# Moving the second graph linear layer into the next iteration, and the first norm's subtract-and-scale from VectorE to GpSimd

## The reference

```python
h = jnp.maximum(_layernorm(x, axis=-1), 0.0)
x = x + _L0_gnn_ref(h, L0_gnn_W, adj)      # qkv = h @ W; softmax(q k / sqrt(32) + mask) @ v
h = jnp.maximum(_layernorm(x, axis=-1), 0.0)
x = x + _L1_gnn_ref(h, adj, ...)
# in _L1_gnn_ref:
h = relu(adj @ (x @ Wg0 + bg0))
h = relu(adj @ (h @ Wg1 + bg1))
for p in range(1, 5):                      # windows of p tokens, an LSTM of p steps with its own weights
    last = _lstm_last(Wih[p - 1], Whh[p - 1], ..., wins)
    h = h.at[:, idx, :].set(last)          # replaces the last token of every window
```

## Time and profile before

| | us |
|---|---|
| median of 3 runs | 555.82 (555.24 to 557.22) |
| the profiled execution, its whole time | 555.92 |
| its span, first to last instruction | 554.1 |
| first phase up to the LSTMs' bulk | about 0 to 302 |
| one iteration of the loop, k = 4 to 13 | 17.58 |
| PE busy, DVE busy, ACT busy, POOL busy in the span | 500.2, 444.8, 352.1, 103.6 |

### The profile page before, as it was taken

The page is one execution under the profiler, slowest core; times in us unless marked ns, Lnnn a source line. Parts: engine busy times, 40 slices in busy tenths (PEclk is TensorE's granted clock), DMA queues, the critical chain, the costliest instruction groups (busy, mean ns, idle before and its releaser), DMA issues.

```text
span 554.1 us, 10019 instructions
## 1 busy us (share of the span) xinstructions
PE 500.2 (90%) x3464; PEld 433.8 (78%) x3464; DVE 444.8 (80%) x974; ACT 352.1 (64%) x573; POOL 103.6 (19%) x123
## 2 busy tenths in 40 slices
PE   3787999999999999999989999999999999999654
PEld 3577888888888888888778778889999988888533
DVE  4777888888888888887775788888788888788896
ACT  2446766677667766687557777777666676655341
POOL 2111110101111110100000012112111212233473
PEclk9989999999999999999999999999999999999975
DMA  7323000000000000000000000000000000000234
GB/s 214 101 82 90 2 2 1 1 0 0 0 0 0 0 0 0 0 0 2 1 0 1 2 0 2 0 0 2 1 1 1 1 0 1 0 2 17 60 95 133
DMA packets 18777, 11.28 MB, mean 20 GB/s; under 512 B 662, under 2 KB 17724, under 8 KB 18748
## 3 DMA queue, kind: packets, MB, share of 16 engines
q1 hardware_dynamic: 17052, 10.03, 6.3%
q10 hardware_dynamic: 1696, 0.87, 0.6%
HBM read 6.70 MB, written 4.19 MB: 20 GB/s over the span
## 4 chain that ended last, share of the span: by engine, by line
PE 52%; DVE 27%; ACT 11%; issue 7%; DMA 2%; DVEq 1%; POOL 0%; ACTq 0%; SPq 0%
PE ps L876 18%; PE ps L814 10%; DVE arena L1179 4%; PE ps L724 4%; DVE rmax L1098 4%; ACT arena L553 4%; DVE S_hi L1173 3%; PE ps L746 3%; PE ps L735 3%; DVE arena L1160 3%; DVE arena L1100 3%; PE ps L756 3%; PE ps L827 2%; PE ps L832 2%; ACT arena L575 2%
## 5 line engine op out<-in xcount | busy, mean ns | idle before, releaser
L589 ACT ACTIVATE arena<-ps,bias 128x512 f32<-128x512 f32 (+1 forms) x207 | 120.7, 625 | 38.3 <-PE ps L876 36.8
L553 ACT ACTIVATE arena<-ps 128x512 f32<-128x512 f32 (+1 forms) x112 | 87.6, 796 | 35.2 <-PE ps L735 20.7
L876 PE MATMUL ps<-H_hi,W_hi 128*128 128x512 f32 (+2 forms) x207 | 76.0, 367 | 6.5 <-DVE S_lo L1175 5.2
L724 PE MATMUL ps<-ident,arena 128*128 128x128 f32 x384 | 55.3, 293 | 29.3 <-ACT arena L558 16.3
L724 PEld LDWEIGHTS ps<-ident,arena 128*128 128x128 f32 x384 | 46.6, 150 | 40.4 <-ACT arena L558 22.8
L814 PEld LDWEIGHTS ps<-arena 128*128 128x128 f32 x512 | 69.0, 193 | 10.6 <-issue 5.3
L533 POOL TENSOR_TENSOR arena<-arena 128x512 f32<-128x512 f32 (+1 forms) x36 | 44.1, 1225 | 168.1 <-ACT arena L589 168.1
L876 PE MATMUL ps<-H_lo,W_hi 128*128 128x512 f32 (+2 forms) x207 | 75.3, 364 | 0.0
L876 PE MATMUL ps<-H_hi,W_lo 128*128 128x512 f32 (+2 forms) x207 | 74.9, 362 | 0.0
L814 PE MATMUL ps<-arena 128*128 128x33 f32 x512 | 66.1, 265 | 3.2 <-ACT arena L553 2.5
L558 ACT ACTIVATE arena<-arena 128x1024 f32<-128x1024 f32 x32 | 34.6, 1081 | 46.9 <-DVE arena L1100 46.9
(11 more groups left out here) (105 smaller groups left out, 1005.8 us busy)
## 6 DMA issues: line engine op xcount, KB each, us to landing
X<-in_x_dram SPq DMA_DIRECT2D x16, 256.0 KB, 2.8
out_dram<-X SPq DMA_DIRECT2D x14, 256.0 KB, 2.3
out_dram<-X ACTq DMA_DIRECT2D x2, 256.0 KB, 3.0
arena<-in_L_gnn_W_dram ACTq DMA_DIRECT2D x1, 128.0 KB, 3.1
wg<-in_L_gnn_Wg_dram ACTq DMA_DIRECT2D x2, 64.0 KB, 2.4
bg_rows<-in_L_gnn_bg_dram SPq DMA_DIRECT2D x6, 0.5 KB
wv<-in_L_gnn_W_dram ACTq DMA_DIRECT2D x1, 64.0 KB, 3.1
adj_sb<-in_adj_dram SPq DMA_DIRECT2D x1, 64.0 KB, 3.3
```

Source lines behind the costliest of these rows:

```text
L553: a_.activation(to, psum, func).then_inc(ready, 1)
L589: a_.activation(to[:, it.buf, 0:w], ps[:, 4 * it.par + j, 0:w], func, bias=bias[:, col:col + 1])\
L724: last = nc.tensor.transpose(to[:, b * P:(b + 1) * P], src[:, b, :], ident[:])
L876: l = mm(o, wt, v, start=m == 0, stop=m == len(terms) - 1)
```

## The change

The second graph linear layer leaves the end of iteration k. It is done in iteration k+1, behind the V and Q projections and ahead of the transposes of the probabilities; `graph_linear_2(g, first)` now takes its group by number. On PE the last gate, `first_gate(s, 2, 3)`, now stands behind `scores()`. On DVE `normalize(0, k+2, ...)` is gone, and its four instructions stand on POOL as `first_norm`, between the two `rsqrt` of an iteration, waiting for the reciprocal root and for the transposes that read `xn` last. DVE's `moments(0, k+2)` waits for `xn_ready` of the group before, because `mv` is now read by POOL. Groups 0 and 1 are still normed on DVE. The POOL program of the first phase is written out for all 18 iterations and holds no loop any more.

```diff
--- before.py
+++ after.py
@@ -505,16 +505,28 @@
                 pool.wait_ge(ve, g + 1)
                 g_.tensor_tensor(rstd[:, layer, :], veps[:, layer, :], minus_half[:], ALU.pow).then_inc(done, 1)
 
+            def first_norm(g):
+
+                pool.wait_ge(rstd1, g + 1)
+
+                pool.wait_ge(xnT_done, g)
+                for b in range(GB):
+                    l = g_.tensor_scalar(xn[:, b, :], X[:, ds(g * GB + b, 1), :].rearrange("p a d -> p (a d)"),
+                                         mv[:, 0, b, 0:1], rstd[:, 0, b:b + 1], ALU.subtract, ALU.mult)
+                l.then_inc(xn_ready, 1)
+
             rsqrt(0, 0, var1, veps1, rstd1)
             rsqrt(0, 1, var1, veps1, rstd1)
 
             def iteration(s):
                 if s.next2:
                     rsqrt(0, s.k + 2, var1, veps1, rstd1)
+                    first_norm(s.k + 2)
                 if s.mid:
                     rsqrt(1, s.k - 1, var2, veps2, rstd2)
 
-            pipeline(pool, iteration)
+            for k in range(GROUPS + 2):
+                iteration(Step(k))
 
             def visit(it, prev):
                 if it and it.t == OUT and it.chunk < CHUNKS[MAX_SKIP] - 1:
@@ -757,12 +769,13 @@
                            start=False, stop=b == GB - 1)
                 return l
 
-            def graph_linear_2(s):
+            def graph_linear_2(g, first):
 
                 def bias():
-                    pe.wait_ge(u2T_ready, s.k - 1)
-                    if s.finish:
-                        pe.wait_ge(first_acts, s.k * 3 - 6)
+                    pe.wait_ge(u2T_ready, g + 1)
+                    if not first:
+
+                        pe.wait_ge(first_acts, g * 3)
                     mm(by_token(psB), bg_parts[:, 1, :], sums_parts[:].unsqueeze(2).to_broadcast([ROWS, N, GB]),
                        start=True, stop=False)
 
@@ -897,6 +910,7 @@
             def last_iteration(s):
 
                 k = s.k
+                interleave([], graph_linear_2(k - 3, False))
                 visit(early[1], early[0])
                 pe.wait_ge(hn2_ready, k - 1)
                 interleave([], graph_mix(hn2, u1_done))
@@ -908,7 +922,7 @@
                 interleave([], graph_mix(h1, u2_done))
                 first_gate(s, 2, 3)
                 visit(early[2], early[1])
-                interleave([], graph_linear_2(s))
+                interleave([], graph_linear_2(k - 2, False))
 
             def iteration(s):
                 k = s.k
@@ -937,6 +951,9 @@
                         transpose_weight(2)
                         pe.wait_ge(sums_ready, 1)
                         transpose_weight(3)
+                if s.finish:
+
+                    interleave([], graph_linear_2(k - 3, not s.after))
                 if s.mid and not s.prep:
                     transpose_prob(s, 0)
                 if s.next1:
@@ -995,20 +1012,17 @@
                 if s.mid:
                     interleave(attend(s, 1), masks)
                 if s.back:
-
                     pe.wait_ge(h1_ready, k - 1)
                     interleave([], graph_mix(h1, u2_done))
-                first_gate(s, 2, 3)
                 if not s.mid:
                     pe.wait_ge(w_lo_done, MAX_SKIP)
                     put_mask((2, 3))
                 if s.front:
                     pe.wait_ge(k_ready, k + 1)
                     scores()
+                first_gate(s, 2, 3)
                 if s.at == GROUPS:
                     visit(early[0], None)
-                if s.back:
-                    interleave([], graph_linear_2(s))
 
             pipeline(pe, iteration)
 
@@ -1263,14 +1277,13 @@
                         split_weight(m)
                 if s.next2:
                     dve.wait_ge(x_loaded, k * 16 + 48)
+
+                    dve.wait_ge(xn_ready, k + 2)
                     moments(0, k + 2, stats1, var1)
                 if s.finish:
                     output_lo(k - 3)
                 if s.after:
                     first_h_part(k - 4)
-                if s.next2:
-                    dve.wait_ge(xnT_done, k + 2)
-                    normalize(0, k + 2, xn, rstd1, xn_ready)
                 if s.mid:
                     over_sums(s, 0)
                 if s.after:
```

## The result

The changed kernel took 550.59 us in the median of four runs (550.14 to 551.06), the kernel before 555.65; the ratio is 0.9888, with a 95% interval from 0.9844 to 0.9931. Measured again later, on one of the two chips where the experiments ran, the same pair gave 550.38 and 556.21, 0.9900 (0.9862 to 0.9938). Faster, then, by 5 to 6 us. The forecast was 551.0. The trace shows that this sum came out right although its two terms did not: the loop gave less than forecast and the start nothing, and the clock, which was at nothing in the sum, gave the rest.

What follows compares the result with a forecast made beforehand. It took a ring through DVE, ACT and PE as the bound, PE's scores ending last by little. From 555.92 us it took 3.5 (gate) and 1.4 (iteration 0): 551.0, own range 549 to 553.5, full range 547.0 to 556.0.

Steps and rivals of the forecast that it cites:

- the clock: Iterations 1 and 16: both falls to 1.2 GHz may vanish, 548.2 us, chance 0.12; or a new one come, 552.4.
- What bounds an iteration: Ahead of the row maximum: PE's scores end last, DVE's statistics could allow a start 0.22 us earlier in the loop.
- The gate behind the scores, 3.5 us: Last gate moved behind PE's scores, 13 shifts: ten loop ones at 0.22 us, three written-out at 0.44; 3.5 in sum.
- the branch: Loop's shift gap: lower bound 0 for the gate's gain if DVE's own registers and loop branch fill it.
- The linear layer's move, 0: Linear layer behind Q, between scores and transposes: same PE work in either order, ACT's read covered by V and Q; cost 0.
- PE's idle time: PE's wait before the transposes of the probabilities in the loop: falls from 0.80 to about 0.58 us.
- The norm off DVE in the loop, 0: DVE loses 1.11 us per loop iteration where it already has slack; the freed time becomes idle, gain 0.
- The price on POOL, 0.40 each: Four norm instructions on POOL: 0.40 us each, 1.6 for four, with 0.29 and 1.01 kept for the range.
- the power: Dearest POOL instruction of the phase, 1.01 us for four columns; kept as the upper end of the norm's price.
- Iteration 0, 1.4 us: Start: without the norm DVE is 2.59 us ahead, PE's transposes come 1.3 to 1.7 earlier; gain 1.4, carried on.
- The blocking rival: Between first half's division and cell part: POOL instructions above 0.69 us block DVE, 570 us; chance 0.10.
- The late norm: Start: POOL's first scalar instruction waits for code not yet there, eating the 1.4 us gain; 555 us, chance 0.06.

Runs made afterwards that it cites:

- the norm alone: Against the kernel before: only the first norm moved to POOL, its program written out, PE's order as before; 557.00 us, ratio 0.9991 (0.9960 to 1.0021).

## Why the prediction was right, and where it wasn't

- **What bounds an iteration**: right. Two branches end side by side, PE's scores last by a little. Both directions were shown, by the gate's move and by writing DVE out in both kernels.
- **The gate behind the scores, 3.5 us**: mechanism right, size 2.8. The three written-out iterations gave 0.44 to 0.48 each, as worked out. Of the ten in the loop I gave each 0.22; six gave 0.18 to 0.24, the four whose next shift stands behind the loop's branch gave 0.03 to 0.06. Together 1.4 + 1.2 + 0.2 = 2.8. The term mis-sized is the branch: I had it only as a bound, and took for DVE's spare time what is its own there. The very row from which I read the 0.22, the shift at 179.61, is one of these four; in the changed kernel its gap is still 0.14.
- **The linear layer's move, 0**: right alone (M 228.45), and right in the loop's steady iterations. Beside the gate's move it is worth 0.7 of the 2.8 us, by covering the 0.78 of ACT's read, in two of the thirteen steps. The prediction said that V and Q cover the read, and priced nothing for it being uncovered. PE's idle time was to be 0.58: it is 0.56 in every second iteration and 0.80 in the others.
- **The norm off DVE in the loop, 0**: right, shown by the norm alone.
- **The price on POOL, 0.40 each**: wrong. 0.79 alone, 1.1 on average. The rows of a cast and of a multiplication were the nearest in kind, and the instruction was twice as dear; the power, kept only as the bound, was the nearer one in price.
- **Iteration 0, 1.4 us**: wrong for that reason alone, -0.14 measured. With half the work on DVE the transposes came at 24.42, where the prediction had them.
- **The blocking rival**: its condition was met and its result didn't come. It was to decide from 0.69 us per instruction; POOL took 1.1, even for six instructions, and M did not move. The step that failed is that DVE would lose what POOL takes. That held in the earlier trace rows for POOL's multiplication with two inputs, where DVE's instruction ended 0.19 behind POOL's, and not for its scalar instruction with one. The Trainium skill (SBUF — State Buffer, "Who interferes with whom") has the engine that issues first hold the shared ports for its whole instruction and the other fully block, when DVE reads in a mode that uses both port pairs, which a scalar instruction can. The trace disagrees: DVE's began later, ended 0.14 before POOL's and lost 0.09; with DVE written out it takes 0.42 beside POOL and loses nothing.
- **The late norm**: POOL's first four took 3.14 us, the next four of the same trace 3.13. A first use of this instruction cost nothing. The Trainium skill (GPSIMD Engine Reference, section 2.1) gives about 6 us for the first call of a freshly loaded kernel; no run here shows such a wait.
- **The clock**: a rival in the prediction with 0.12, and it came true in the first comparison: the missing falls gave 1.0 and about 1.1 us. They made up almost to the tenth for what the two wrong terms lacked: 2.8 - 0.14 + 2.1 = 4.8, where 3.5 + 1.4 = 4.9 was forecast. The sum was right by that luck. The fewer falls themselves are no accident of one execution, eight of ten of the changed kernel are without them; but the prediction had no reason for that, and the runs don't give one either.

## What to carry to other kernels

Where two engines' branches join, look at which one's instruction ends last and by how much, to the tenth of a microsecond: that margin is all that a reordering on the later engine can give, and then the other branch is the bound, here with DVE's register and branch work in it. Read the margin at every kind of iteration, since one behind a loop's branch can differ from one inside its body. Work taken off an engine that waits later in the same ring gives nothing; look for the place where the engine stands on the chain, and there ask what the new engine takes for it. And a total that agrees with a forecast is no proof of its terms: compare marks inside the trace.

## What the runs showed of the hardware

A GpSimd subtract-and-multiply with per-partition scalars on 128x128 float32 takes 0.79 us alone and 0.95 to 1.82 where DVE works beside it, against 0.28 on DVE (four in 1.11). DVE's instructions beside it lengthen by 0.09 at most. DVE's loop adds 0.28 us to an iteration of 17.10 and 0.45 where the branch stands in it: by registers for addresses ahead of the sum and of the statistics, some 0.13 each, and by the branch, some 0.2. TensorE's granted clock was at 0.50 for 0 to 20 us of the first 60 us, differently in executions of the same kernel, and for 21 to 24 us of the last 31; this moves single times by several us. It stays at 1.00 through all of the loop.
